# Value products of a sliding-window attention: high and low half of the probabilities in one product of 320 columns, with their results added by VectorE

## Chip, cores and metric

The kernel runs on one core of a Trainium2 chip. The metric is the device time of one launch in microseconds. Six queues of instructions matter: TensorE (PE, with its weight loads as PEld), VectorE (DVE), ScalarE (ACT), GpSimd (POOL) and SyncE (SP), which issues all transfers. They run side by side and wait for each other by semaphores.

## The reference, cut to what matters

The input is 32 sequences of 256 rows of 128 numbers. After a layer norm, two branches are computed and added to the input.

```
h = relu(x @ nm_w1 + nm_b1);  m = h @ nm_w2 + nm_b2
q, k, v = m @ q_w + q_b, m @ k_w + k_b, m @ v_w + v_b
scores = einsum('bsd,bswd->bsw', q, k_band) * scale      # window of 65 rows, 32 to each side
weights = softmax(where(valid, scores, -inf))
attn = einsum('bsw,bswd->bsd', weights, v_band)
combine = top 8 of 16 sigmoid gates, normalised, times 2.826
ffn = sum_e combine[e] * (silu(x @ w_gate[e]) * (x @ w_up[e])) @ w_down[e]  +  shared expert
out = x + attn + ffn
```

## The kernel before

**Tiles.** The 8192 rows are worked in 16 groups of 512 rows, two sequences each. Activations lie turned, 128 features on the partitions and 512 rows on the columns. Every operand of a large product is split in a high part (`_hi`, rounded by ScalarE) and a low part (`_lo`, the rest, by VectorE), and a product is three: hi by hi, lo by hi, hi by lo (`PAIRS3`).

**Slots.** Groups are counted from 0. A group has 17 slots, one for the shared expert and each of the 16 experts. `program` calls `slot(g, par, s)` on every engine in the same order, so the order on an engine is that of its code. In a slot TensorE does `gate_proj` of the next expert into `ps_g`, `down` of the expert three back (`LAG`) into `ps_y`, and `up_proj` of this one into `ps_u`, nine products of 512 columns. ScalarE applies silu (L717), GpSimd multiplies it by the routing weight (`silu_c`, L1257), VectorE multiplies this into `ps_u` (`h_prod`, L1132), ScalarE makes `h_hi` (L725) and VectorE `h_lo` (L1138). `h_prod`, `h_hi` and `h_lo` of an expert are worked in the slot after its own. There are two banks of `ps_u`: `up_proj` of slot s waits for `h_lo` of slot s-2.

**Attention in the slots.** `att_early`, `att_late` and `att` put one piece of the attention in fixed slots. Keys and values need no own projections: the products go to the hidden tile, and value weights are applied after. `hid_n_hi` and `hid_n_lo` (slots 0 and 1) are its two parts with rows on the partitions, reloaded from memory (`store_hid`, `load_hid`; `hid_blocks` in slot 12 of the group before makes the blocks that are stored). `scores` is in slots 3 and 5, the turned probabilities (`prob_hi`, `prob_lo`) are ready in slots 7 to 10. `attend(0)` and `attend(1)` in slots 13 and 14 multiply the hidden tile by them; both sequences of a group write one bank, `bank[2]`. `z_hi` (ScalarE, slot 15) and `z_lo` (VectorE, slot 16) split the result, and `value_proj` adds its product with the value weights to `ps_y` in slot 0 of the next group, or ahead of the last three `down` calls in `finish`.

**What else touches this place.** On VectorE `q_lo` of the next group stands between `z_lo` and `h_lo` of slot 15; the first use of its result is `turn` or `scores` in slots 1 to 3. In slot 1 `hid_n_lo` subtracts two tiles in SBUF. In slot 3 `finish_group` (L1014) reads `ps_y` of the group before, adds the input and signals `s_y_out`; `down` of the new group's first expert, in TensorE's slot 3, waits for that, since it overwrites `ps_y`:

```python
if s == 0 and not first(g):
    pe.wait_ge(s_y_out, g)
```

Of the kernel before, what the change touches and what calls it, by code (L numbers as in the profile page):

```python
# [12 lines left out]
P = 128  # L13
# [59 lines left out]
def layer(nc, x, x_t, watt, watt_t, expert_bias, wexp, out_t, c_dram, st_dram, h_dram):  # L73
    ctx = ExitStack()
    with ctx:
        def sb(name, shape, dt=F32):
            return ctx.enter_context(nc.sbuf_tensor(name, shape, dt))
# [4 lines left out]
        def sem(name):  # L82
# [53 lines left out]


        prob_n = sb("prob_n", [P, NB, 3 * P])
        p_t = [sb("p_hi", [P, NB, 2, SEQ], F32R), sb("p_lo", [P, NB, 2, WIN], F32R)]

# [24 lines left out]
        ps_y = pb("ps_y")  # L167
        bank = [pb(f"bank{i}") for i in range(3)]
        score_bank = [bank[2], bank[1]]


        s_watt_in = sem("watt_loaded")
# [48 lines left out]
            hid_b gate_1 score select top8 rest weight wsum winv comb comb_t  # L221
            hid_mm hid hid_hi hid_lo q_mm q_hi q_lo hid_tp hn_hi hn_lo key_term
            mask_k sc0 sc1 nmax0 nmax1 exp0 exp1 inv0 inv1 pn0 pn1 pt0 pt1
            p0_hi p0_lo p1_hi p1_lo pv z_hi z_lo""".split()
        S = {n: sem(n) for n in names}
        s_hid_st = sem("hid_stored")
        s_hid_m = sem("hid_loaded")
# [20 lines left out]
        def last(g, ahead=0):  # L248
            return g >= GROUPS - 1 - ahead
# [8 lines left out]

        def flat(t):
            return t[:].rearrange("p a d -> p (a d)")  # L260

        def windows(b):

            return b[:, 0:2 * APART].rearrange("p (t c) -> p t c", t=2)[:, :, 0:WIN]
# [139 lines left out]
        def _(pe):  # L404
# [36 lines left out]

            def attend(seq):

                for kb in range(2):
                    col = seq * SEQ + kb * (P - HALF)
                    for n, (a, b) in enumerate(PAIRS3):
                        wide = SEQ if kb == 0 and n == 0 else WIN
                        done = mm(bank[2][:, col:col + wide], hid_n[a][:, seq * 2 + kb, :],  # L448
                                  p_t[b][:, seq, kb, 0:wide], start=kb == 0 and n == 0, stop=kb == 1 and n == 2,
                                  skip_group_check=True)  # L450
                return done

            def value_proj(g):

                pe.wait_ge(S["z_lo"], g + 1)
                for a, b in PAIRS3:
                    mm(ps_y[:], att_w[a][:, 2, :], z_t[b][:], start=False, stop=False, skip_group_check=True)  # L457
# [154 lines left out]
            def att_late(g, par, s):  # L612

                if s == 0 and not first(g):
                    value_proj(g - 1)
                if s == when(g, 9, 12):
                    pe.wait_ge(S["pn1"], g + 1)
                    turn_probs(1)
                if s == 13:
                    pe.wait_ge(S["hn_lo"], g + 1)  # L620
                    pe.wait_ge(S["p0_lo"], g + 1)
                    attend(0)
                if s == 14:
                    pe.wait_ge(S["p1_lo"], g + 1)
                    attend(1).then_inc(S["pv"], 1)

            def slot(g, par, s):
# [19 lines left out]
                        hid_proj(g + 1, 1 - par)  # L647

            def finish():
                value_proj(GROUPS - 1)  # L650
                for s in range(STEPS - LAG, STEPS):
                    down(GROUPS - 1, (GROUPS - 1) % 2, s)

            program(prologue, slot, finish)

        @block.scalar
        def _(act):
# [39 lines left out]

            def z_hi(g):
                act.wait_ge(S["pv"], g + 1)
                A(z_t[0][:], bank[2][:], ACT.Copy).then_inc(S["z_hi"], 1)  # L700

            def prob_exp(g, seq):
                act.wait_ge(S[f"nmax{seq}"], g + 1)
# [5 lines left out]

            def prob_hi(g, seq):  # L710
                act.wait_ge(S[f"pt{seq}"], g + 1)
                A(p_t[0][:, seq, :, 0:WIN], windows(score_bank[seq]), ACT.Copy).then_inc(S[f"p{seq}_hi"], 1)

            def gate_silu(g, par, s):
                i = (par + s) % 2
# [101 lines left out]
        def _(dve):  # L817
# [149 lines left out]

            def z_lo(g):
                dve.wait_ge(S["z_hi"], g + 1)
                V.tensor_tensor(z_t[1][:], bank[2][:], z_t[0][:].bitcast(F32), ALU.subtract).then_inc(S["z_lo"], 1)  # L970

            def prologue():
                V.memset(spin_in[:].bitcast(F32), 0.0).then_inc(s_spin, 1)
                V.memset(prob_n[:], 0.0)
                V.memset(p_t[0][:, :, 0, WIN:SEQ].bitcast(F32), 0.0)
                moments(0, 0)
                variance(0)
                dve.wait_ge(s_gatew_hi, 1)
                V.tensor_tensor(gate_w[:, :, E:2 * E], gate_raw, gate_w[:, :, 0:E].bitcast(F32),
                                ALU.subtract).then_inc(s_gatew, 1)  # L980
                normalise(0, 0)
                xn_lo(0, 0)
                dve.wait_ge(s_attw_hi, 1)
                V.tensor_scalar(vecs[:, 0:1], bank[2][:, M_VEC:M_VEC + 1], att_raw[:, QB:QB + 1], SCALE,
                                ALU.add, ALU.mult)
                V.tensor_scalar(vecs[:, 3:4], bank[2][:, M_VEC + 1:M_VEC + 2], att_raw[:, KB:KB + 1], SCALE,
                                ALU.add, ALU.mult)
                V.tensor_tensor(vecs[:, 1:3], bank[2][:, M_VEC + 1:M_VEC + 3], att_raw[:, KB:VB + 1], ALU.add)\
                    .then_inc(s_vec1, 1)
                V.tensor_tensor(att_w[1][:, 0, :], att_raw[:, W1:W1 + P], att_w[0][:, 0, :].bitcast(F32),  # L990
                                ALU.subtract)
                V.tensor_tensor(att_w[1][:, 2, :], bank[2][:, M_V:M_V + P], att_w[0][:, 2, :].bitcast(F32),
                                ALU.subtract).then_inc(s_attw, 1)
                gate_sum(0)
                route_scores(0)
                route_max(0)
                route_match(0)
                route_sum(0)
                route_weights(0, 0)

                dve.wait_ge(s_side, 1)
                V.tensor_copy(vecs[:, 4:7], ps_u[1][:, M_VEC + 4:M_VEC + 7]).then_inc(s_vec2, 1)
# [35 lines left out]

            def prob_lo(g, seq):
                dve.wait_ge(S[f"p{seq}_hi"], g + 1)  # L1040
                V.tensor_tensor(p_t[1][:, seq, :, :], windows(score_bank[seq]),
                                p_t[0][:, seq, :, 0:WIN].bitcast(F32), ALU.subtract).then_inc(S[f"p{seq}_lo"], 1)

            def att(g, par, s):
                more = not last(g)
# [52 lines left out]
                        hid_lo(g + 1)  # L1098
                if s == 16:
                    z_lo(g)  # L1100
                    if more:
                        q_lo(g + 1)

            def fresh_att(s):

# [35 lines left out]
            def slot(g, par, s):  # L1141
                some = not first(g) or s > 0
                if s == 3 and not first(g):
                    finish_group(g - 1, 1 - par)
                if s == when(g, 6, 9):
                    row_max(g, 1)
                if first(g) and s == 3:
                    score_weights()
                if some:
                    h_prod(*before(g, par, s))  # L1150
                att(g, par, s)
                if some:
                    h_lo(*before(g, par, s))
                if first(g) and s == 1:
                    moments(1, 1)

            def finish():
                h_prod(GROUPS - 1, (GROUPS - 1) % 2, STEPS - 1)
# [153 lines left out]
```

## Time and profile before

| | |
|---|---|
| median of 3 runs | 691.51 us (691.34 to 692.12) |
| the profiled execution | 691.06 us |
| its span | 689.2 us |
| mean granted TensorE clock | 0.997 |
| PE busy | 678.9 us, 98% |
| DVE busy | 596.4 us, 87% |
| ACT busy | 438.2 us, 64% |
| POOL busy | 443.2 us, 64% |

Busy shares are averages over the span. The end of a product is modelled, and consecutive ones overlap in the record: a product of 512 columns is listed with 0.39 us though the next starts 0.23 us after it. So starts are compared, not durations. The same holds for VectorE, where an operation of 512 columns is listed with 0.68 us and the next starts after 0.60.

### The profile page before, as it was taken

Reading aid. Unit: us, or ns where it says so; the run is one execution under the profiler, and the core shown is the slowest. Engines: PE = TensorE matmul, PEld = TensorE weight load, DVE = VectorE, ACT = ScalarE, POOL = GpSimd, SP = SyncE. Lnnn points to the kernel's source line nnn. Section 1 sums busy time; section 2 is a strip of 40 time slices with the busy share of each in tenths; the row PEclk is TensorE's granted clock in tenths of the full one; section 3 lists DMA queues with packets and bytes.
Section 4 is the critical chain, followed back from the end, with each engine's and each line's share of the span. In section 5 each row is a group of like instructions: output and inputs, shape, how many; then the busy total and the mean of one; then the engine's idle time right before and its main releaser. Section 6 shows DMA issues by size and latency. Waiting matters only on the chain.

```text
span 689.2 us, 10454 instructions
## 1 busy us (share of the span) xinstructions
PE 678.9 (98%) x3172; PEld 554.3 (80%) x3172; DVE 596.4 (87%) x1640; ACT 438.2 (64%) x874; POOL 443.2 (64%) x400
## 2 busy tenths in 40 slices
PE   8989999999999999999999999999999999999997
PEld 6768788888888888888888888888888888888886
DVE  7998889988898888889988898888889988888775
ACT  5765665757566566665757566576665757566573
POOL 5774567567666766667567666766667567666553
PEclk9999999999999999999999999999999999999999
DMA  8506246171542626245171643626245161631500
GB/s 268 230 0 250 89 144 225 38 270 62 197 172 94 237 70 248 90 146 223 39 271 62 211 159 92 239 70 263 75 148 221 39 270 46 211 128 63 230 0 16
DMA packets 38040, 101.80 MB, mean 148 GB/s; under 512 B 8672, under 2 KB 18144, under 8 KB 29920
## 3 DMA queue, kind: packets, MB, share of 16 engines
q1 hardware_dynamic: 37984, 101.14, 40.6%
q8 instruction: 25, 0.41, 0.3%
q14 instruction: 31, 0.25, 0.1%
HBM read 92.42 MB, written 8.70 MB: 147 GB/s over the span
## 4 chain that ended last, share of the span: by engine, by line
PE 88%; DVE 5%; ACT 2%; DMA 2%; issue 1%; POOL 0%; SPq 0%; DVEq 0%; ACTq 0%
PE ps_y L487 25%; PE ps_u L477 25%; PE ps_g L467 25%; PE bank L409 3%; PE bank L448 3%; PE bank L431 3%; PE ps_y L457 1%; PE bank L438 1%; DVE ps_u L1132 1%; PE bank L420 1%; DMA h_dram<-exp_raw 1%; PE ps_u L509 1%; DVE h_lo L1138 1%; ACT h_hi L725 1%; ACT silu L717 0%
## 5 line engine op out<-in xcount | busy, mean ns | idle before, releaser
L1257 POOL TENSOR_TENSOR silu_c<-silu,comb_b 128x512 f32<-128x512 f32 x252 | 325.3, 1293 | 226.3 <-ACT silu L717 225.3
L725 ACT ACTIVATE h_hi<-ps_u 128x512 fp32r<-128x512 f32 x272 | 162.6, 598 | 236.1 <-DVE ps_u L1132 236.1
L1138 DVE TENSOR_TENSOR h_lo<-ps_u,h_hi 128x512 fp32r<-128x512 f32 x272 | 185.6, 682 | 40.6 <-ACT h_hi L725 34.7
L1132 DVE TENSOR_TENSOR ps_u<-silu_c,ps_u 128x512 f32<-128x512 f32 x256 | 175.9, 687 | 28.2 <-PE ps_u L477 24.2
L717 ACT ACTIVATE silu<-ps_g 128x512 f32<-128x512 f32 x272 | 161.9, 595 | 0.2
L477 PE MATMUL ps_u<-xn_hi,exp_w_hi 128*128 128x512 f32 x272 | 111.1, 408 | 2.9 <-DVE h_lo L1138 2.8
L487 PE MATMUL ps_y<-h_hi,exp_w_hi 128*128 128x512 f32 x272 | 109.5, 403 | 1.0 <-DVE h_lo L1138 0.4
L467 PE MATMUL ps_g<-xn_hi,exp_w_hi 128*128 128x512 f32 x272 | 108.2, 398 | 0.8 <-ACT silu L717 0.7
L487 PE MATMUL ps_y<-h_lo,exp_w_hi 128*128 128x512 f32 x272 | 107.8, 396 | 0.0
L477 PE MATMUL ps_u<-xn_hi,exp_w_lo 128*128 128x512 f32 x272 | 107.5, 395 | 0.0
L487 PE MATMUL ps_y<-h_hi,exp_w_lo 128*128 128x512 f32 x272 | 107.2, 394 | 0.0
L467 PE MATMUL ps_g<-xn_hi,exp_w_lo 128*128 128x512 f32 x272 | 106.9, 393 | 0.0
L477 PE MATMUL ps_u<-xn_lo,exp_w_hi 128*128 128x512 f32 x272 | 106.6, 392 | 0.0
L467 PE MATMUL ps_g<-xn_lo,exp_w_hi 128*128 128x512 f32 x272 | 105.9, 389 | 0.0
L477 PEld LDWEIGHTS ps_u<-xn_hi,exp_w_hi 128*128 128x128 f32 x272 | 51.1, 188 | 16.7 <-DVE h_lo L1138 5.5
L467 PEld LDWEIGHTS ps_g<-xn_hi,exp_w_hi 128*128 128x128 f32 x272 | 51.1, 188 | 13.5 <-issue 1.1
L487 PEld LDWEIGHTS ps_y<-h_hi,exp_w_lo 128*128 128x128 f32 x272 | 51.3, 189 | 12.4
L467 PEld LDWEIGHTS ps_g<-xn_hi,exp_w_lo 128*128 128x128 f32 x272 | 51.1, 188 | 12.5
L467 PEld LDWEIGHTS ps_g<-xn_lo,exp_w_hi 128*128 128x128 f32 x272 | 51.3, 188 | 12.2
L477 PEld LDWEIGHTS ps_u<-xn_hi,exp_w_lo 128*128 128x128 f32 x272 | 51.1, 188 | 12.2
L487 PEld LDWEIGHTS ps_y<-h_hi,exp_w_hi 128*128 128x128 f32 x272 | 51.3, 189 | 11.4 <-DVE h_lo L1138 0.8
L487 PEld LDWEIGHTS ps_y<-h_lo,exp_w_hi 128*128 128x128 f32 x272 | 51.4, 189 | 9.9
(156 smaller groups left out, 987.8 us busy)
## 6 DMA issues: line engine op xcount, KB each, us to landing
comb_b<-c_dram SPq DMA_DIRECT2D x63, 1024.0 KB, 7.2
mom_b<-st_dram SPq DMA_DIRECT2D x13, 512.0 KB, 3.7
xres<-x_t SPq DMA_DIRECT2D x16, 256.0 KB, 2.5
out_t<-xres SPq DMA_DIRECT2D x16, 256.0 KB, 2.0
xin<-x SPq DMA_DIRECT2D x15, 256.0 KB, 3.1
h_dram<-exp_raw SPq DMA_DIRECT2D x60, 64.0 KB
exp_raw<-h_dram SPq DMA_DIRECT2D x15, 256.0 KB, 3.1
xn<-x_t SPq DMA_DIRECT2D x13, 256.0 KB, 3.4
```

The source lines that it names most:

```text
L409: done = mm(dst[:], att_w[a][:, w, :], parts[b][:], start=n == 0, stop=n == 2)
L420: done = mm(bank[0][:], gate_w[:].rearrange("p q c -> p (q c)"), xn_t[par][n][:], start=n == 0, stop=n == 1)
L431: done = mm(dst[:, t * SEQ:t * SEQ + WIN], q_t[a][:, q0:q0 + P], hid_t[b][:, k0:k0 + WIN], start=n == 0, stop=n == 2)
L448: done = mm(bank[2][:, col:col + wide], hid_n[a][:, seq * 2 + kb, :], p_t[b][:, seq, kb, 0:wide], start=kb == 0 and n == 0, stop=kb == 1 a ...
L467: done = mm(ps_g[i][:], exp_w[a][:, s, 0:P], xn_t[par][b][:], start=n == 0, stop=n == 2)
L477: done = mm(ps_u[i][:], exp_w[a][:, s, P:2 * P], xn_t[par][b][:], start=n == 0, stop=n == 2)
L487: done = mm(ps_y[:], exp_w[a][:, s, 2 * P:3 * P], h_t[i][b][:], start=s == 0 and n == 0, stop=s == STEPS - 1 and n == 2, skip_group_check= ...
L717: A(silu[i][:], ps_g[i][:], ACT.Silu).then_inc(s_silu, 1)
L725: A(h_t[hbuf(par, s)][0][:], ps_u[(par + s) % 2][:], ACT.Copy).then_inc(s_h_hi, 1)
L1132: V.tensor_tensor(ps_u[i][:], src[:], ps_u[i][:], ALU.mult).then_inc(s_h, 1)
L1138: V.tensor_tensor(t[1][:], ps_u[(par + s) % 2][:], t[0][:].bitcast(F32), ALU.subtract)\
L1257: G.tensor_tensor(silu_c[i][:], silu[i][:], comb_b[:, s1 - 1, :], ALU.mult).then_inc(s_silu_c, 1)
```

## The change

Both halves of the probabilities now lie in one tile, `p_t[:, half, sequence, block, :]`. In `attend`, the high part of the hidden tile is multiplied by both halves in one product of 2 x 160 columns. The result of the low half goes to columns 256 to 511 of the same bank, beside that of the high half. The low part of the hidden tile is multiplied by the high half as before. So each sequence needs a bank of its own (`att_bank`), and the second one waits for `hid_hi` of the next group, which reads `bank[0]`. The first product is no longer widened to 256 columns over zeros. ScalarE copies z in two pieces. VectorE subtracts in two pieces, waits for itself, and adds the other half in two more. `q_lo` of the next group moves from between `z_lo` and `h_lo` to the end of slot 16. In `finish`, `value_proj` goes behind the first of the last three `down` calls.

```diff
-        p_t = [sb("p_hi", [P, NB, 2, SEQ], F32R), sb("p_lo", [P, NB, 2, WIN], F32R)]
+        p_t = sb("p_t", [P, 2, NB, 2, WIN], F32R)
...
+        att_bank = [bank[2], bank[0]]
...
+        def halves(b):
+            return b[:].rearrange("p (h t) -> p h t", h=2)
...
             def attend(seq):
+                dst = att_bank[seq]
                 for kb in range(2):
-                    col = seq * SEQ + kb * (P - HALF)
-                    for n, (a, b) in enumerate(PAIRS3):
-                        wide = SEQ if kb == 0 and n == 0 else WIN
-                        done = mm(bank[2][:, col:col + wide], hid_n[a][:, seq * 2 + kb, :],
-                                  p_t[b][:, seq, kb, 0:wide], start=kb == 0 and n == 0, stop=kb == 1 and n == 2,
-                                  skip_group_check=True)
+                    c = slice(kb * (P - HALF), kb * (P - HALF) + WIN)
+                    mm(halves(dst)[:, :, c], hid_n[0][:, seq * 2 + kb, :], p_t[:, :, seq, kb, :],
+                       start=kb == 0, stop=False, skip_group_check=True)
+                    done = mm(dst[:, c], hid_n[1][:, seq * 2 + kb, :], p_t[:, 0, seq, kb, :],
+                              start=False, stop=kb == 1, skip_group_check=True)
...
                 if s == 14:
                     pe.wait_ge(S["p1_lo"], g + 1)
+                    pe.wait_ge(S["hid_hi"], g + 1 + (not last(g)))
                     attend(1).then_inc(S["pv"], 1)
...
             def finish():
-                value_proj(GROUPS - 1)
                 for s in range(STEPS - LAG, STEPS):
                     down(GROUPS - 1, (GROUPS - 1) % 2, s)
+                    if s == STEPS - LAG:
+                        value_proj(GROUPS - 1)
...
             def z_hi(g):
                 act.wait_ge(S["pv"], g + 1)
-                A(z_t[0][:], bank[2][:], ACT.Copy).then_inc(S["z_hi"], 1)
+                for seq in range(NB):
+                    done = A(z_t[0][:, seq * SEQ:(seq + 1) * SEQ], att_bank[seq][:, 0:SEQ], ACT.Copy)
+                done.then_inc(S["z_hi"], 1)
...
             def z_lo(g):
                 dve.wait_ge(S["z_hi"], g + 1)
-                V.tensor_tensor(z_t[1][:], bank[2][:], z_t[0][:].bitcast(F32), ALU.subtract).then_inc(S["z_lo"], 1)
+                for seq in range(NB):
+                    c = slice(seq * SEQ, (seq + 1) * SEQ)
+                    done = V.tensor_tensor(z_t[1][:, c], att_bank[seq][:, 0:SEQ], z_t[0][:, c].bitcast(F32),
+                                           ALU.subtract)
+                done.then_inc(S["z_rest"], 1)
+                dve.wait_ge(S["z_rest"], g + 1)
+                for seq in range(NB):
+                    c = slice(seq * SEQ, (seq + 1) * SEQ)
+                    done = V.tensor_tensor(z_t[1][:, c], att_bank[seq][:, SEQ:2 * SEQ], z_t[1][:, c].bitcast(F32),
+                                           ALU.add)
+                done.then_inc(S["z_lo"], 1)
...
-                V.memset(p_t[0][:, :, 0, WIN:SEQ].bitcast(F32), 0.0)
...
                 if s == 16:
                     z_lo(g)
-                    if more:
-                        q_lo(g + 1)
...
+                if s == STEPS - 1 and not last(g):
+                    q_lo(g + 1)
```

On TensorE, one call of `attend` in slot 13 stands like this before, between the last product of `down` and the first of `up_proj`:

```order
L487 MATMUL ps_y<-h_hi,exp_w_lo 128x512
L448 MATMUL bank<-p_hi,hid_n_hi 128x256 [waits p0_lo,hn_lo]
L448 MATMUL bank<-p_lo,hid_n_hi 128x160
L448 MATMUL bank<-p_hi,hid_n_lo 128x160
L448 MATMUL bank<-p_hi,hid_n_hi 128x160
L448 MATMUL bank<-p_lo,hid_n_hi 128x160
L448 MATMUL bank<-p_hi,hid_n_lo 128x160
L477 MATMUL ps_u<-xn_hi,exp_w_hi 128x512 [waits h_lo_ready]
```

In the changed kernel the same place on TensorE is this:

```order
L495 MATMUL ps_y<-h_hi,exp_w_lo 128x512
L455 MATMUL bank<-p_t,hid_n_hi 128x2x160 [waits p0_lo,hn_lo]
L457 MATMUL bank<-p_t,hid_n_lo 128x160
L455 MATMUL bank<-p_t,hid_n_hi 128x2x160
L457 MATMUL bank<-p_t,hid_n_lo 128x160
L485 MATMUL ps_u<-xn_hi,exp_w_hi 128x512 [waits h_lo_ready]
```

Six products became four, two of them of 2 x 160 columns; nothing else moved past them.

On VectorE, the end of a group (slot 16) and the first operation of the next stand like this before; the products named `ps_u<-silu_c,ps_u` are `h_prod`:

```order
L1132 TENSOR_TENSOR ps_u<-silu_c,ps_u 128x512 [waits silu_c_ready,up_prod_ready]
L970 TENSOR_TENSOR z_lo<-bank,z_hi 128x512 [waits z_hi]
L929 SCALAR_TENSOR_TENSOR q_lo<-bank,vecs,q_hi 128x512 [waits q_hi]
L1138 TENSOR_TENSOR h_lo<-ps_u,h_hi 128x512 [waits h_hi_ready]
L1132 TENSOR_TENSOR ps_u<-silu_c,ps_u 128x512 [waits silu_c_ready,up_prod_ready]
```

In the changed kernel:

```order
L1152 TENSOR_TENSOR ps_u<-silu_c,ps_u 128x512 [waits silu_c_ready,up_prod_ready]
L985 TENSOR_TENSOR z_lo<-bank,z_hi 128x256 [waits z_hi]
L985 TENSOR_TENSOR z_lo<-bank,z_hi 128x256
L991 TENSOR_TENSOR z_lo<-bank,z_lo 128x256 [waits z_rest]
L991 TENSOR_TENSOR z_lo<-bank,z_lo 128x256
L1158 TENSOR_TENSOR h_lo<-ps_u,h_hi 128x512 [waits h_hi_ready]
L942 SCALAR_TENSOR_TENSOR q_lo<-bank,vecs,q_hi 128x512 [waits q_hi]
L1152 TENSOR_TENSOR ps_u<-silu_c,ps_u 128x512 [waits silu_c_ready,up_prod_ready]
```

One operation became four, and `q_lo` went behind `h_lo`, but is still ahead of the next `h_prod`.

## Rows read from the trace of the kernel before

**Rows 1.** The page's first part: busy time of each engine.

```profile
PE 678.9 (98%) x3172; PEld 554.3 (80%) x3172; DVE 596.4 (87%) x1640; ACT 438.2 (64%) x874; POOL 443.2 (64%) x400
```

**Rows 2.** Waits: us in total, times, longest us.

```profile
PE ps_u L477 <- DVE h_lo L1138: 2.8, 4, 1.9
```

**Rows 3.** Timeline of PE, group 6, slot 13: start us, duration us, instruction.

```profile
302.95 0.39 PE L487 MATMUL ps_y<-h_hi,exp_w_lo 128*128 128x512 f32 x1
303.18 0.28 PE L448 MATMUL bank<-p_hi,hid_n_hi 128*128 128x256 f32 x1
303.30 0.23 PE L448 MATMUL bank<-p_lo,hid_n_hi 128*128 128x160 f32 x1
...
303.71 0.28 PE L448 MATMUL bank<-p_hi,hid_n_lo 128*128 128x160 f32 x1
303.82 0.43 PE L477 MATMUL ps_u<-xn_hi,exp_w_hi 128*128 128x512 f32 x1
304.08 0.39 PE L477 MATMUL ps_u<-xn_lo,exp_w_hi 128*128 128x512 f32 x1
```

**Rows 4.** Timeline of ACT, group 1, slot 0: idle time ahead, in brackets.

```profile
66.16 0.63 ACT L696 ACTIVATE hid_n_hi<-exp_raw 128x512 fp32r<-128x512 f32 x1 [2.05 <-DMA exp_raw<-h_dram]
```

**Rows 5.** Timeline of DVE, slot 16 of group 6 to slot 3 of group 7.

```profile
310.29 0.69 DVE L1132 TENSOR_TENSOR ps_u<-silu_c,ps_u 128x512 f32<-128x512 f32 x1 [0.73 <-PE ps_u L477]
310.89 0.68 DVE L970 TENSOR_TENSOR z_lo<-bank,z_hi 128x512 fp32r<-128x512 f32 x1
311.49 0.74 DVE L929 SCALAR_TENSOR_TENSOR q_lo<-bank,vecs,q_hi 128x512 fp32r<-128x512 f32 x1
312.15 0.68 DVE L1138 TENSOR_TENSOR h_lo<-ps_u,h_hi 128x512 fp32r<-128x512 f32 x1
312.75 0.68 DVE L1132 TENSOR_TENSOR ps_u<-silu_c,ps_u 128x512 f32<-128x512 f32 x1
...
315.15 0.70 DVE L1132 TENSOR_TENSOR ps_u<-silu,ps_u 128x512 f32<-128x512 f32 x1 [0.36 <-PE ps_u L477]
315.76 0.77 DVE L949 TENSOR_TENSOR hid_n_lo<-exp_raw,hid_n_hi 128x512 fp32r<-128x512 f32 x1
...
317.00 0.68 DVE L1138 TENSOR_TENSOR h_lo<-ps_u,h_hi 128x512 fp32r<-128x512 f32 x1
...
319.56 0.74 DVE L1014 SCALAR_TENSOR_TENSOR xres<-ps_y,vecs,xres 128x512 f32<-128x512 f32 x1
```

**Rows 6.** Line L1041, a narrower operation: duration ns min/median/max.

```profile
L1041 DVE TENSOR_TENSOR p_lo<-bank,p_hi x32: 472/476/482, 50.9 to 668.2; 128x320 fp32r<-128x320 f32 x32
```

**Rows 7.** Timeline and line L949: GpSimd's product, and subtractions in SBUF.

```profile
304.59 1.30 POOL L1257 TENSOR_TENSOR silu_c<-silu,comb_b 128x512 f32<-128x512 f32 x1 [0.61 <-ACT silu L717]
...
305.35 1.09 DVE L924 TENSOR_TENSOR hid_lo<-hid,hid_hi 128x512 fp32r<-128x512 f32 x1
...
314.70 1.29 POOL L1257 TENSOR_TENSOR silu_c<-silu,comb_b 128x512 f32<-128x512 f32 x1 [1.85 <-ACT silu L717]
...
L949 DVE TENSOR_TENSOR hid_n_lo<-exp_raw,hid_n_hi x15: 691/780/787, 66.8 to 646.5; 128x512 fp32r<-128x512 f32 x15
```

**Rows 8.** Timeline of PE, slots 2 and 3: first products of up_proj and down(0).

```profile
318.44 0.40 PE L477 MATMUL ps_u<-xn_hi,exp_w_hi 128*128 128x512 f32 x1
...
320.46 0.43 PE L487 MATMUL ps_y<-h_hi,exp_w_hi 128*128 128x512 f32 x1
```

**Rows 9.** Timeline of group 1, slot 3: the same place where PE waited.

```profile
70.54 0.74 DVE L1014 SCALAR_TENSOR_TENSOR xres<-ps_y,vecs,xres 128x512 f32<-128x512 f32 x1
...
71.33 0.51 PE L487 MATMUL ps_y<-h_hi,exp_w_hi 128*128 128x512 f32 x1 [0.34 <-DVE xres L1014]
```

**Rows 10.** Timeline of the last 10 us.

```profile
681.53 0.68 DVE L970 TENSOR_TENSOR z_lo<-bank,z_hi 128x512 fp32r<-128x512 f32 x1
...
682.29 0.69 DVE L1138 TENSOR_TENSOR h_lo<-ps_u,h_hi 128x512 fp32r<-128x512 f32 x1
...
684.99 0.50 PE L487 MATMUL ps_y<-h_hi,exp_w_hi 128*128 128x512 f32 x1 [0.37 <-DVE h_lo L1138]
```

More of the change, by code:

```diff
@@ L223, in layer @@
             mask_k sc0 sc1 nmax0 nmax1 exp0 exp1 inv0 inv1 pn0 pn1 pt0 pt1
-            p0_hi p0_lo p1_hi p1_lo pv z_hi z_lo""".split()
+            p0_hi p0_lo p1_hi p1_lo pv z_hi z_rest z_lo""".split()
         S = {n: sem(n) for n in names}
@@ L711, in prob_hi @@
                 act.wait_ge(S[f"pt{seq}"], g + 1)
-                A(p_t[0][:, seq, :, 0:WIN], windows(score_bank[seq]), ACT.Copy).then_inc(S[f"p{seq}_hi"], 1)
+                A(p_t[:, 0, seq, :, :], windows(score_bank[seq]), ACT.Copy).then_inc(S[f"p{seq}_hi"], 1)
             def gate_silu(g, par, s):
@@ L1040, in prob_lo @@
                 dve.wait_ge(S[f"p{seq}_hi"], g + 1)
-                V.tensor_tensor(p_t[1][:, seq, :, :], windows(score_bank[seq]),
-                                p_t[0][:, seq, :, 0:WIN].bitcast(F32), ALU.subtract).then_inc(S[f"p{seq}_lo"], 1)
+                V.tensor_tensor(p_t[:, 1, seq, :, :], windows(score_bank[seq]),
+                                p_t[:, 0, seq, :, :].bitcast(F32), ALU.subtract).then_inc(S[f"p{seq}_lo"], 1)
             def att(g, par, s):
```

## The prediction

> **What bounds the kernel now.** I read the page's busy times, then the waits, then the timeline. TensorE is busy 98% of the span [rows 1], and its second-most frequent direct wait, that of up_proj for h_lo, is 2.8 us in four places [rows 2]. So in nearly every group TensorE's own queue sets the time, and a microsecond taken out of that queue is one gained, as long as VectorE, ScalarE and GpSimd, which prepare its operands, keep their lead. The prediction is therefore two questions: what the value products cost TensorE, and how much of VectorE's lead the longer z work uses up.
>
> **Value products.** One call of attend, in group 6, starts at 303.18. The first product after it starts at 303.82, and the second at 304.08 [rows 3]. A product of 512 columns has a pitch (start to start) of 0.23 there (302.95 to 303.18) [rows 3], so the call costs 304.08 - 303.18 - 0.23 = 0.67 us. Its 256-column product has a pitch of 0.12, and a 160-column one 0.11 (303.71 to 303.82) [rows 3], although by columns it should be 0.07: each product loads its own weights, and these loads follow each other no faster. After the change a call is 320, 160, 320, 160 columns. A 320-column product is in no row; between 256 columns at 0.12 and 512 at 0.23 it comes to 0.145 (an estimate). The 160-column ones stay at 0.11. So a call costs 2 x (0.145 + 0.11) = 0.51, and saves about 0.155 us. Bounds: 0.12 for the wide product (the narrower row) saves 0.21 per call, and 0.23 (the wider row) saves nothing. I take the straight line, since the two rows differ by their columns alone.
>
> The Trainium skill (TensorE: Matmul & The Clock Gate, Back-to-back issue gap) gives an isolated product N/2.4 + 2.5 ns. By that alone a call would go from 0.46 to 0.41 and save 0.045 us. The row has 0.67 for the call, so here the loads count too, which the same section says of a stream of loads and products.
>
> Thirty-two calls are made. The two of group 0 I count at nothing: in group 1, slot 1, ScalarE waits 2.05 us for the reloaded hidden tile, from memory [rows 4], whose transfer hangs on hid_blocks in slot 12, ahead of those calls, and TensorE waits behind it. Gain: 30 x 0.155 = 4.7 us.
>
> **The z block on VectorE (slot 16).** Before, it is one subtraction of 512 columns with a pitch of 0.60 (310.89 to 311.49) and a duration of 0.68, then q_lo with a pitch of 0.66 [rows 5]. After, it is four of 256 columns, the third waiting for the second to end. A 320-column operation of the same kind lasts 476 ns [rows 6] against 683, so 256 columns last about 0.41, with a pitch of 0.33 (the overlap of 0.08 with the next stays). The block is 0.33 + 0.41 + 0.03 + 0.33 + 0.33 = 1.43; 0.03 is the own semaphore, an estimate below the 0.05 that TensorE takes after VectorE's end [rows 9]. That is +0.83 per group. Bounds: each of the four at the 320-column pitch of 0.40 gives +1.11, and at half the 512-column pitch, 0.30, gives +0.71. The z copies of ScalarE become two; z_lo at 310.89 finds them done, so they hide.
>
> q_lo moves behind h_lo(15). So h_lo(15) starts only 0.17 later, well before its reader, but h_prod(16) at 312.75 is behind both and starts 0.83 later, at 313.58. q_lo's reader, scores(0) in slot 3, is far off. The memset of p_hi that goes from the prologue is counted at nothing, since VectorE waits for x there.
>
> **Where the 0.83 goes.** Before slot 16's z block VectorE had waited 0.73 for TensorE [rows 5], so up to there it keeps step with the faster TensorE. From h_prod(16) on, everything is late by 0.83: h_hi(16), then silu(1) behind it on ScalarE, then GpSimd's silu_c(1) at 314.70, whose idle time ScalarE's silu ended [rows 7]. VectorE itself had 0.36 idle before h_prod(0) at 315.15 [rows 5] and would win back 0.45 there (the overlap of 0.08 too). But hid_n_lo follows, with both inputs in SBUF, and it doesn't run beside GpSimd's product: it lasts 0.77 from 315.76 to 316.53, which is 0.54 after GpSimd's end at 315.99. hid_lo shows the same: 1.09 long, its end at 306.44 is 0.55 after GpSimd's end at 305.89. Alone, hid_n_lo lasts 691 ns at its least [rows 7]. So its end is tied to GpSimd's end and not to its own start: it is late by the full 0.83, and with it the VectorE queue behind it.
>
> The Trainium skill (SBUF — State Buffer, Who interferes with whom) says that a VectorE instruction with two SBUF inputs and a GpSimd one that reads SBUF block each other fully, first come first served. By that rule the delay passes on, as by these rows.
>
> **What TensorE then waits for.** h_lo(0) starts at 317.00 [rows 5]; late by 0.83 and 0.68 long it ends at 318.51. up_proj(2) waits for it, started at 318.44 [rows 8], and can start at 318.56: 0.12 late. A product that had to wait is also longer, 0.51 in the waiting case [rows 9] against 0.40 [rows 8], since its weights came late: 0.23 in all. Then finish_group, which must read ps_y before down(0) of the new group may overwrite it: xres starts at 319.56 and takes 0.74 [rows 5], so it ends at 320.30, and down(0) starts at 320.46 [rows 8]. With 0.05 for the semaphore the lead is 0.11 us. Late by 0.83, xres ends at 321.13, down(0) starts at 321.18, 0.72 later than now, and with 0.51 for 0.43 the loss is 0.80 (the earlier 0.23 is in it, since both count from the same delayed queue). Group 1 shows this wait already: xres at 70.54, down(0) at 71.33, 0.34 idle [rows 9]; there VectorE was free for want of the transfer, which hides the 0.83. That leaves the 14 boundaries before groups 2 to 15. After slot 4 TensorE, itself late, is waited for again, and nothing is carried into the next group. Loss: 14 x 0.80 = 11.2 us.
>
> **The end.** The last group has no q_lo. z_lo starts at 681.53 and h_lo(15) at 682.29 [rows 10]; after, 681.53 + 1.43 = 682.96. h_prod(16), h_hi(16), h_lo(16) and the last down follow in line (it waits 0.37 for h_lo at 684.99 [rows 10]): +0.67. value_proj behind the first down has cover until then.
>
> **Sum.** -4.7 + 11.2 + 0.7 = +7.2 us. The profiled execution took 691.06 (span 689.2), the median of the three runs is 691.51, 0.45 above it, so the run becomes 698.3 and the median 698.7 us, 1.0% slower.
>
> **Rivals.**
> - *The delay isn't inherited through GpSimd.* If hid_n_lo runs beside silu_c(1), VectorE wins back 0.45 at h_prod(0) and is late by 0.38. Then up_proj(2) doesn't wait, and down(0) loses 0.38 - 0.11 + 0.08 = 0.35. Sum: -4.7 + 4.9 + 0.7 = +0.9, 692.4 us. Against it are 14 stretched hid_n_lo. Chance 0.12.
> - *Faster.* VectorE's delay at finish_group stays under the lead of 0.11 us. It decides there and nowhere else: below it no boundary costs anything and the products' gain is left, -4.7 + 0.7 = -4.0, 687.5 us. For it: VectorE is idle 13% of the span, some of it in slots 1 to 4, and the price of a 256-column operation is read from wider ones. Against it: even at the lower bound of +0.71 and with 0.45 won back, 0.26 is left. Chance 0.13.
> - *The wide product saves nothing.* Two separate stretches of 160 columns in one product could cost as two, 0.22. A call is then 0.66, the gain is nil: +11.9, 703.4 us. Nothing in the trace reads or writes columns in two such pieces on TensorE at this width, so it isn't excluded. Chance 0.12. By the skill's gap alone, the gain would be 30 x 0.045 = 1.4 and the time 702.
> - *The forecast*, one boundary loss near 0.8 and a call near 0.51: chance 0.6. Its own range is 696 to 702: the bounds of the z block move it by -0.12 x 14 = -1.7 and +0.28 x 14 = +3.9, those of the product by -1.7.
> - 0.03 for something above all of these.
>
> **Chances.** A difference under 0.2%, 1.4 us, can't be told from none: 690.1 to 692.9. Faster is the second rival, 0.13. Same is the first rival, most of it, 0.10. Slower is the rest, 0.77. The range leaves out the faster case and the extreme ends: 692.0 to 703.5.
>
> **What the profile after would show.** (1) attend: starts 0.145 and 0.11 apart, a call at 0.51. (2) Four z operations near 410 ns, h_prod(16) 0.83 later against the up_proj(16) before it. (3) hid_n_lo stretched from 0.77 to about 1.2. (4) In the waits, TensorE at ps_y's first product for xres in 15 groups, where it is one now, and for h_lo at up_proj(2); the step from up_proj(2) to down(0) longer. (5) The last wait for h_lo near 1.0 in place of 0.37. It would be wrong if hid_n_lo's end isn't tied to GpSimd, if the delay is taken up before slot 3 by some idle time that I didn't count, or if the 320-column product isn't priced by its columns.

## The result, and the profile after

| | before | changed |
|---|---|---|
| median | 691.55 us (691.34 to 692.12, 4 runs) | 713.19 us (712.66 to 713.32, 4 runs) |
| span of the profiled execution | 689.2 us | 710.8 us |
| granted TensorE clock | 0.997 | 0.997 |

The changed kernel is slower by 3.1%: the ratio is 1.031, 95% interval 1.0292 to 1.0328. The forecast was 698.7 us, range 692.0 to 703.5. The direction was right, and the loss is three times as large as forecast.

The page's first part, after, against [rows 1]: TensorE's busy time hardly moved, VectorE's rose by 32.5 us (the page shows rounded shares).

```profile
PE 680.9 (96%) x3108; PEld 549.9 (77%) x3108; DVE 628.9 (88%) x1687; ACT 439.0 (62%) x890; POOL 442.1 (62%) x400
```

The waits after, against [rows 2]: us in total, times, longest us. The wait of `up_proj` for `h_lo` had 2.8 us in 4 places, and the one of `down` for `xres` is now in 15 groups.

```profile
PEld ps_u L485 <- DVE h_lo L1158: 26.3, 23, 2.3
PE ps_u L485 <- DVE h_lo L1158: 16.9, 17, 1.9
PEld ps_y L495 <- DVE xres L1036: 7.3, 15, 0.5
PE ps_y L495 <- DVE xres L1036: 5.0, 15, 0.3
```

The timeline of TensorE after, group 6, slot 13, the place of [rows 3]. A 320-column product has a pitch of 0.14 and 0.19, a 160-column one of 0.07. The call, counted as before, is 311.49 - 310.74 - 0.23 = 0.52 us (0.51 forecast, 0.67 before).

```profile
310.51 0.39 PE L495 MATMUL ps_y<-h_hi,exp_w_lo 128*128 128x512 f32 x1
310.74 0.31 PE L455 MATMUL bank<-p_t,hid_n_hi 128*128 128x320 f32 x1
310.88 0.23 PE L457 MATMUL bank<-p_t,hid_n_lo 128*128 128x160 f32 x1
310.95 0.35 PE L455 MATMUL bank<-p_t,hid_n_hi 128*128 128x320 f32 x1
311.14 0.24 PE L457 MATMUL bank<-p_t,hid_n_lo 128*128 128x160 f32 x1
311.21 0.44 PE L485 MATMUL ps_u<-xn_hi,exp_w_hi 128*128 128x512 f32 x1
311.49 0.39 PE L485 MATMUL ps_u<-xn_lo,exp_w_hi 128*128 128x512 f32 x1
```

VectorE's timeline after, slot 16 of group 6 to slot 3 of group 7, as [rows 5]. From `h_prod(15)` at 317.51 to `h_prod(16)` at 320.82 are 3.31 us, 2.46 before: +0.85, forecast +0.83. `hid_n_lo` lasts 1.24, forecast "about 1.2". What wasn't forecast is the second `key_prod` behind it, 1.36 us long; the first took 0.34.

```profile
317.51 0.70 DVE L1152 TENSOR_TENSOR ps_u<-silu_c,ps_u 128x512 f32<-128x512 f32 x1 [0.72 <-PE ps_u L485]
318.11 0.75 DVE L985 TENSOR_TENSOR z_lo<-bank,z_hi 128x256 fp32r<-128x256 f32 x2
318.90 0.76 DVE L991 TENSOR_TENSOR z_lo<-bank,z_lo 128x256 fp32r<-128x256 f32 x2
...
320.82 0.69 DVE L1152 TENSOR_TENSOR ps_u<-silu_c,ps_u 128x512 f32<-128x512 f32 x1
...
322.78 0.68 DVE L1152 TENSOR_TENSOR ps_u<-silu,ps_u 128x512 f32<-128x512 f32 x1
323.38 1.24 DVE L962 TENSOR_TENSOR hid_n_lo<-exp_raw,hid_n_hi 128x512 fp32r<-128x512 f32 x1
324.54 0.34 DVE L975 CUSTOM_DVE_ANT_0 key_prod<-exp_raw,key_row,vecs 128x128 f32<-128x128 f32 x1
...
324.81 1.36 DVE L975 CUSTOM_DVE_ANT_0 key_prod<-exp_raw,key_row,vecs 128x128 f32<-128x128 f32 x1
...
326.10 0.68 DVE L1158 TENSOR_TENSOR h_lo<-ps_u,h_hi 128x512 fp32r<-128x512 f32 x1
...
327.57 0.34 DVE L975 CUSTOM_DVE_ANT_0 key_prod<-exp_raw,key_row,vecs 128x128 f32<-128x128 f32 x1
...
328.05 0.69 DVE L1158 TENSOR_TENSOR h_lo<-ps_u,h_hi 128x512 fp32r<-128x512 f32 x1
328.66 0.74 DVE L1036 SCALAR_TENSOR_TENSOR xres<-ps_y,vecs,xres 128x512 f32<-128x512 f32 x1
```

GpSimd's timeline in the same stretch shows what stands beside both; that it is the cause is for the experiments to show. `silu_c(1)` ends at 324.06 and `hid_n_lo` 0.56 after it. `silu_c(2)` starts at 324.66, 0.15 ahead of the second `key_prod` and 0.12 behind the first; it ends at 326.02, and the stretched one at 326.17.

```profile
322.77 1.29 POOL L1279 TENSOR_TENSOR silu_c<-silu,comb_b 128x512 f32<-128x512 f32 x1 [2.71 <-ACT silu L730]
324.66 1.36 POOL L1279 TENSOR_TENSOR silu_c<-silu,comb_b 128x512 f32<-128x512 f32 x1 [0.60 <-ACT silu L730]
```

TensorE's timeline at the two places of [rows 8], both without a wait before:

```profile
326.84 0.50 PE L485 MATMUL ps_u<-xn_hi,exp_w_hi 128*128 128x512 f32 x1 [1.01 <-DVE h_lo L1158]
...
329.46 0.50 PE L495 MATMUL ps_y<-h_hi,exp_w_hi 128*128 128x512 f32 x1 [0.33 <-DVE xres L1036]
```

I worked out a table from the same timelines: the step from the start of one slot's `up_proj` to the next, median over groups 4 to 14, and its difference to the kernel before, in us. It is used for every run below. Slots that aren't listed differ by 0.01 at most in this run.

| step | before | changed | |
|---|---|---|---|
| slot 1 to 2 | 2.087 | 3.270 | +1.183 |
| slot 2 to 3 | 2.761 | 3.428 | +0.667 |
| slot 12 to 13 | 2.720 | 2.563 | -0.157 |
| slot 13 to 14 | 2.753 | 2.587 | -0.166 |
| group | 41.347 | 42.865 | +1.518 |

The account of the spans closes: -0.37 up to the start of group 2, 13 groups up to that of group 15 +19.77, group 15 to its last `up_proj` +1.51, from there to the end +0.69. Sum +21.6, and 710.8 - 689.2 = 21.6.

### The profile page after: what moved, and what is told of

Same layout as the page of the kernel before. It is cut to its first block, busy times and chain, and to the rows that moved or that the text cites. A ratio compares the mean times of both kernels' runs of the same rounds, so it can differ in the third digit from the quotient of the medians.

```text
span 710.8 us, 10405 instructions
## 1 busy us (share of the span) xinstructions
PE 680.9 (96%) x3108; PEld 549.9 (77%) x3108; DVE 628.9 (88%) x1687; ACT 439.0 (62%) x890; POOL 442.1 (62%) x400
## 4 chain that ended last, share of the span: by engine, by line
PE 65%; DVE 22%; issue 6%; ACT 5%; DMA 2%; POOL 0%; SPq 0%; DVEq 0%; ACTq 0%
PE ps_y L495 19%; PE ps_u L485 19%; PE ps_g L475 17%; DVE ps_u L1152 6%; DVE key_prod L975 3%; ACT h_hi L738 3%; PE bank L417 3%; DVE h_lo L1158 2%; DVE xres L1036 2%; DVE q_lo L942 2%; DVE hid_n_lo L962 1%; DVE z_lo L985 1%; PE bank L455 1%; PE bank L446 1%; PE bank L439 1%
## 5 line engine op out<-in xcount | busy, mean ns | idle before, releaser
L485 PE MATMUL ps_u<-xn_hi,exp_w_hi 128*128 128x512 f32 x272 | 112.7, 414 | 17.2 <-DVE h_lo L1158 16.9
```

The lines of the kernel that those rows point to most:

```text
L485: done = mm(ps_u[i][:], exp_w[a][:, s, P:2 * P], xn_t[par][b][:], start=n == 0, stop=n == 2)
```

## The experiments

Theory A: VectorE operations that can't run beside GpSimd's product turn 0.85 us of delay into 1.9, and the gain of the products is there but smaller. Theory B has a different explanation in each run, given there. Theory C: the larger amount of VectorE work alone makes the loss. Every run was timed beside runs of the kernel before, and its ratio is to these; intervals are 95%.

### The z block alone, and the products alone

`e1_z_block_only` is the kernel before with VectorE's part of the change; the additions go to a tile that nobody reads, so their work stands but not their result.

```diff
+                done.then_inc(S["z_rest"], 1)
+                dve.wait_ge(S["z_rest"], g + 1)
...
+                    done = V.tensor_tensor(z_pad[:, c], bank[2][:, c], z_t[1][:, c].bitcast(F32), ALU.add)
...
+                if s == STEPS - 1 and not last(g):
+                    q_lo(g + 1)
```

> The kernel before with VectorE's side of the change alone: z_lo in two subtractions of 256 columns, the own wait, two additions of 256 columns (into a scratch tile, so the result stays), and q_lo behind h_lo(15). The value products stay the six of before. Theory A (the longer z block makes VectorE late, and GpSimd's products then stand in the way of its operations with two SBUF inputs in slot 1): all of the loss and none of the gain, 713.2 + 4.7 = about 717.9 us. Rival B (the loss comes from the products, the second bank or its wait on hid_hi): near the kernel before, at most 692.4 to 698.7 us.

Measured: 718.33 us (717.98 to 718.92), ratio 1.0381 [1.0366, 1.0397]. All of the loss is here (14 x 1.85 + 0.7 = 26.6 us by the steps), with nothing changed on TensorE or ScalarE. That rules out the new products, the second bank and the wait for `hid_hi` as its cause.

`e2_no_addition` is the changed kernel without the two additions and their wait; the low half's contribution to z is left out.

```diff
-                done.then_inc(S["z_rest"], 1)
-                dve.wait_ge(S["z_rest"], g + 1)
...
-                    V.tensor_tensor(z_t[1][:, c], att_bank[seq][:, SEQ:2 * SEQ], z_t[1][:, c].bitcast(F32),
-                                           ALU.add)
```

> The changed kernel without the two additions of z's low half (the low half of the probabilities doesn't reach the result) and without the wait between. TensorE's and ScalarE's side stay. Theory A: the z block has a pitch of 0.67 in place of 0.60, nothing is late, and the gain of the products stands alone, 691.5 - 4.7 = about 687 us. Rival B (products, bank or the wait on hid_hi): stays above 700 us.

Measured: 688.77 us (688.71 to 690.5), ratio 0.9961 [0.9947, 0.9975]. Its steps are -0.157 and -0.166 in slots 13 and 14, as in the changed kernel, and +0.134 from slot 2 to 3: the two pieces and the moved `q_lo` still make VectorE late enough for `xres`. That remainder is 14 x 0.134 = 1.9 us, and it is why this run isn't at 687.

### The same work, met by GpSimd at another time

`e3_q_lo_slot0` moves `q_lo` behind `h_lo(16)` in slot 0. VectorE does the same work up to `xres`.

```diff
-                if s == STEPS - 1 and not last(g):
-                    q_lo(g + 1)
+                if s == 0 and not first(g):
+                    q_lo(g)
```

> The changed kernel with q_lo of the next group moved from the end of slot 16 to the end of slot 0, behind h_lo(16). VectorE's work is the same. h_prod(16), ScalarE's silu(1) and GpSimd's silu_c(1) are then late by about 0.2 us and not 0.85, while hid_n_lo starts as late as now. Theory A: hid_n_lo no longer waits for GpSimd, the key products go through before silu_c(2), h_lo(0) is late by 0.3 us, down(0) costs about 0.3 us at 14 boundaries: about 691.5 us. Rival C (the amount of VectorE's work between slot 16 and slot 3 sets it, whatever GpSimd does): as the changed kernel, 713 us.

Measured: 691.23 us (690.91 to 691.96), ratio 0.9992 [0.9983, 1.0001]. 22 us are gone with one operation moved by a slot. `hid_n_lo` begins 0.05 us ahead of the end of GpSimd's product and lasts 0.69, and the key products last 0.35. Left is +0.277 from slot 2 to 3. `xres` comes 0.31 later than before, and this remainder is what the amount of work costs. So theory C is ruled out for the 22 us.

`e5_half_silu_c` is the changed kernel with GpSimd's product of experts 1 and 2 on half of the columns (the other half of the columns of these two experts' contribution is left out).

```diff
-                    G.tensor_tensor(silu_c[i][:], silu[i][:], comb_b[:, s1 - 1, :], ALU.mult).then_inc(s_silu_c, 1)
+                    n = T // 2 if s1 <= 2 else T
+                    G.tensor_tensor(silu_c[i][:, 0:n], silu[i][:, 0:n], comb_b[:, s1 - 1, 0:n], ALU.mult)\
+                        .then_inc(s_silu_c, 1)
```

> The changed kernel with GpSimd's silu_c product of experts 1 and 2 of each group cut to 256 columns (the other half of the columns keeps old values, so the result is not the reference's). VectorE, ScalarE and TensorE do all that they did. Theory A: hid_n_lo ends 0.55 after GpSimd's shorter product, the second key product meets no GpSimd product, h_lo(0) comes 1.5 us earlier, TensorE waits only 0.3 us at down(0): about 691.5 us. Rival C (VectorE's own work sets it): 713 us, since nobody waits for these two GpSimd products.

Measured: 691.49 us (690.95 to 691.78), ratio 0.9991 [0.9982, 1.0001]. VectorE's program is untouched, and about 22 us go when GpSimd's operation is shorter. It lasts 0.74 in place of 1.30 and `hid_n_lo` ends 0.55 earlier than in the changed kernel (medians against `up_proj(0)`), though it starts where it did; the key products last 0.34. Left is +0.279 from slot 2 to 3. VectorE didn't wait for GpSimd's result as an operand: that wait is 4.0 us in 15 places in the kernel before and in the changed one alike.

### Only the key product out of the way

`e6_key_slot2` puts the first two key products in slot 2, and the mask terms on GpSimd that read them one slot later. `e10_key_slot2_alone` has only the first pair of lines below and leaves the mask terms in slot 2.

```diff
-                if s == when(g, 1, 5):
+                if s == when(g, 2, 5):
                     key_terms(g, 0)
-                if s == when(g, 2, 5):
+                if s == when(g, 3, 5):
                     mask_terms(g, 0)
```

> The changed kernel with the first pair of key products in slot 2 instead of slot 1 (and the mask terms that read it one slot later), so that no key product stands where GpSimd's next product begins. VectorE's operations are the same and as many; up to xres in slot 3 the same work lies before it. Theory A (the second key product is locked out by GpSimd's product of expert 2, 1.36 in place of 0.34, and this was missing in my sum): the key products last 0.34 each, only hid_n_lo stays stretched at about 1.24, VectorE is late by about 0.83 as forecast, and the time is near the forecast's, 696 to 701 us. Theory C (VectorE's amount of work alone makes the loss): xres comes as late as before this edit and the time stays at 713 us.

Measured: 717.10 us (716.73 to 717.47), ratio 1.0372 [1.0354, 1.0389], outside both expectations. My edit had brought a wait of its own, that of `row_max` in slot 4 for the mask:

```profile
DVE prob L1045 <- POOL mask_k L1263: 30.1, 15, 2.0
```

The steps separate it: 0.000 from slot 1 to 2, where the changed kernel has +1.183, +0.644 from slot 2 to 3, and then +0.403, +0.535, +0.256, +0.011, +0.022 and +0.082 in slots 5 to 11. So I ran it again without that wait.

> As the run with the first key products in slot 2, but with GpSimd's mask terms left in slot 2, so that row_max doesn't wait for them. That run's steps of TensorE from up_proj to up_proj (medians over groups 4 to 14, against the kernel before) were 0 from slot 1 to 2, where the changed kernel has +1.18, +0.64 from slot 2 to 3, and +1.2 in slots 5 to 10, where row_max waited 2.0 us for the mask. Theory A: the last of these goes and the others stay, so a group is -0.33 + 0.64 = +0.31 against before, 14 x 0.31 + 0.7 at the end = +5.0: 695 to 698 us, which is the forecast's own case. Theory C (amount of work): 713 us.

Measured: 696.26 us (696.2 to 696.47), ratio 1.0069 [1.0054, 1.0084]. The steps are -0.001 from slot 1 to 2 and +0.638 from slot 2 to 3. With the key product out of the way of GpSimd's next one, the change costs +4.7 us in place of +21.6. That is close to the forecast's case, but not the same, since two key products have also moved behind `h_prod(1)`. `hid_n_lo` is as stretched as ever (duration ns min/median/max), and the wait for `xres` is TensorE's only new one:

```profile
L962 DVE TENSOR_TENSOR hid_n_lo<-exp_raw,hid_n_hi x15: 692/1247/1249, 67.1 to 651.1; 128x512 fp32r<-128x512 f32 x15
```

```profile
PEld ps_y L495 <- DVE xres L1036: 8.9, 15, 0.9
...
PE ps_y L495 <- DVE xres L1036: 6.6, 15, 0.8
```

### Two doses of delay in the kernel before

One VectorE operation of 128 or of 384 columns is added ahead of `z_lo`, in every group but the last.

```diff
+                if not last(g):
+                    V.tensor_tensor(z_pad[:, 0:128], bank[2][:, 0:128], z_t[0][:, 0:128].bitcast(F32), ALU.add)
                 V.tensor_tensor(z_t[1][:], bank[2][:], z_t[0][:].bitcast(F32), ALU.subtract).then_inc(S["z_lo"], 1)
```

> The kernel before with one extra operation of 128 columns on VectorE ahead of z_lo in slot 16 of every group but the last, written to a tile that nobody reads: a delay of about 0.2 us (an estimate: below the 0.33 of 256 columns). The second key product then still begins ahead of GpSimd's next product (316.73 + 0.2 against 317.05). Theory A: only the lead at xres of 0.11 is used up, 14 x (0.2 - 0.11 + 0.08) = 2.4, 693 to 695.5 us, and no key product is stretched. Theory B (a delay at VectorE costs a multiple of itself wherever it is put): 14 x 0.2 x 2.2 = 6, 697 us or more.

> The same with 384 columns, a delay of about 0.46 us (between 0.40 for 320 and 0.60 for 512 columns). The second key product would begin at 317.19, behind GpSimd's product at 317.05. Theory A: there is a step between the two doses, not a slope: the key product is locked out and gains a further 1.0 us of delay, 14 x (0.46 + 1.02 - 0.11 + 0.1) = 20.6, 708 to 713 us. Theory B (a slope): 14 x (0.46 - 0.11 + 0.08) = 6.0, 697 to 699 us if it costs once, 705 if it costs twice.

| | delay of `h_prod(16)` | step 1 to 2 | step 2 to 3 | us | ratio |
|---|---|---|---|---|---|
| 128 columns | 0.20 | 0.000 | +0.179 | 694.30 | 1.0040 [1.0025, 1.0055] |
| 384 columns | 0.46 | +0.814 | +0.664 | 712.76 | 1.0305 [1.0287, 1.0322] |

The delays are medians of the starts against the same group's `up_proj(0)`. The first 0.20 us cost 2.7 us, and 0.26 more cost 18.5, of which a plain delay of 0.26 in 14 groups would be 3.6. The lines of `hid_n_lo` and `key_prod` (ns min/median/max) with 128 columns:

```profile
L950 DVE TENSOR_TENSOR hid_n_lo<-exp_raw,hid_n_hi x15: 691/990/991, 67.3 to 649.5; 128x512 fp32r<-128x512 f32 x15
```

```profile
L963 DVE CUSTOM_DVE_ANT_0 key_prod<-exp_raw,key_row,vecs x60: 336/344/350, 67.9 to 652.4; 128x128 f32<-128x128 f32 x60
```

and the timelines of VectorE and of GpSimd there, group 6:

```profile
275.64 0.99 DVE L950 TENSOR_TENSOR hid_n_lo<-exp_raw,hid_n_hi 128x512 fp32r<-128x512 f32 x1
...
276.83 0.34 DVE L963 CUSTOM_DVE_ANT_0 key_prod<-exp_raw,key_row,vecs 128x128 f32<-128x128 f32 x1
```

```profile
274.78 1.30 POOL L1260 TENSOR_TENSOR silu_c<-silu,comb_b 128x512 f32<-128x512 f32 x1 [2.05 <-ACT silu L718]
276.94 1.39 POOL L1260 TENSOR_TENSOR silu_c<-silu,comb_b 128x512 f32<-128x512 f32 x1 [0.86 <-ACT silu L718]
```

With 384 columns, the same two timelines:

```profile
282.46 0.34 DVE L963 CUSTOM_DVE_ANT_0 key_prod<-exp_raw,key_row,vecs 128x128 f32<-128x128 f32 x1
...
282.73 1.38 DVE L963 CUSTOM_DVE_ANT_0 key_prod<-exp_raw,key_row,vecs 128x128 f32<-128x128 f32 x1
```

```profile
282.58 1.38 POOL L1260 TENSOR_TENSOR silu_c<-silu,comb_b 128x512 f32<-128x512 f32 x1 [0.59 <-ACT silu L718]
```

At 128 columns the second key product begins 0.11 ahead of GpSimd's product and lasts 0.34. At 384 it begins 0.15 behind it and lasts 1.38. That is a step, no slope: in all 14 groups of the first run the second key product lasts 0.34 or 0.35, in all 14 of the other 1.37 or 1.38.

### Towards a better version

`e7_hid_n_lo_slot4` moves `hid_n_lo` to slot 4, `e8_both_moved` does this and the edit of `e3_q_lo_slot0`, `e9_before_hid_n_lo_slot4` does it in the kernel before. `e11_three_moved` adds to `e8_both_moved` the second pair of key products in slot 3 and its mask terms in slot 4.

```diff
-                if s == when(g, 1, 4):
-                    hid_n_lo(g)
...
+                if s == when(g, 4, 4):
+                    hid_n_lo(g)
```

> The changed kernel with hid_n_lo in slot 4 instead of slot 1 (its only reader is attend in slot 13). q_lo stays in slot 16, so the 0.83 us of delay goes into slot 0 as it does now. Theory A (the delay costs TensorE only through the operations that exclude GpSimd's product, and through the lead at xres): without hid_n_lo the key products run at 0.34 or one is stretched by a few tenths, xres is no later than in the kernel before, both waits at the boundary go or stay below 0.2 us, and the gain of the value products shows: 686 to 690 us. Theory C (the delay at h_prod(16) itself costs, whatever stands in slot 1): 14 boundaries still lose some 0.8 each, 698 us or more.

> The changed kernel with q_lo at the end of slot 0 and hid_n_lo in slot 4: the candidate for a version that beats both. With q_lo alone moved 691.23 us was measured, with a wait of TensorE for xres left at each boundary (0.13 to 0.14 between two products longer than without it, and a late weight load). Theory A: with hid_n_lo out of the way that wait goes too and TensorE's queue alone is left, 684 to 688 us. If the time stays at 691, the wait at the boundary has another cause than VectorE's work ahead of xres.

> The kernel before with hid_n_lo in slot 4 alone: what the lead of 0.11 us at xres and the stretched hid_n_lo cost the kernel before. By its trace TensorE waited for xres in one group only, so theory A expects almost nothing, 690 to 691.5 us; the distance to the run with both moved is then the pure worth of the value products, 30 x about 0.155 = 4.7 us less what is left of the z block at the end (0.7). If this run falls by several us too, the kernel before was held by VectorE more than its waits view shows.

> The version with q_lo in slot 0 and hid_n_lo in slot 4 (689.13 us), and in addition the second pair of key products in slot 3 and its mask terms in slot 4. In the version's trace the step of TensorE from slot 2 to 3 was still 0.087 longer than in the kernel before, with a key product of 0.77 in slot 2. Theory A: this goes, 14 x 0.087 = 1.2 us, 687.5 to 688.5 us. If instead TensorE waits somewhere in slots 3 to 5 for VectorE, it stays at 689 or more.

| | us | ratio | steps that differ from before (slots 13 and 14 apart; above 0.01) |
|---|---|---|---|
| e7 | 693.64 | 1.0031 [1.0017, 1.0044] | 2 to 3 +0.164, 7 to 8 +0.190, 8 to 9 +0.012, 9 to 10 +0.022, 10 to 11 +0.086 |
| e8 | 689.13 | 0.9964 [0.9952, 0.9976] | 2 to 3 +0.087 |
| e9 | 691.93 | 1.0003 [0.9994, 1.0013] | none |
| e11 | 690.90 | 0.9990 [0.9980, 0.9999] | 7 to 8 +0.082, 8 to 9 +0.014, 9 to 10 +0.023, 10 to 11 +0.089 |

`e8_both_moved` is the changed kernel's products with a schedule that bears them: 2.5 us below the kernel before. That is a smaller gain than the 684 to 688 I expected. A wait for `xres` was left, since a key product of slot 2 is stretched to 0.77 us; of the products' 14 x 0.332 = 4.6 us, 14 x 0.087 = 1.2 and the end's 0.7 go off, which leaves 2.7.

`e7_hid_n_lo_slot4` missed its range: its `hid_n_lo` lasts 1.17 in slot 4, again beside a GpSimd product, and there is a new loss in slots 7 to 11. That the one makes the other isn't shown: `e11_three_moved` has steps in the same slots with a `hid_n_lo` of 0.68. `e9_before_hid_n_lo_slot4`, at 0.4 us above its range, gains nothing, although `down(0)` now starts 0.42 after the end of `xres` in place of 0.15: the kernel before had no loss there. `e11_three_moved` missed its range by 2.4 us: it did remove the step from slot 2 to 3, as expected, but lost in slots 7 to 11, where `up_proj` waits for `h_lo` in more places (weight loads 21 times, 8 in `e8_both_moved`). Which of VectorE's operations makes these late was not tested.

## Why the prediction was right in direction and wrong in size

- **The products: right.** A call at 0.52 against 0.51. The steps from slot 12 to 15 give 0.157 + 0.166 + 0.009 = 0.332 a group, 4.6 us in 14 groups; forecast 0.31 a group and 4.7 in all. The pitches inside the call were off, and the closeness of the sum is partly luck: the narrow products have 0.07 and not 0.11, the wide ones 0.14 and 0.19 and not 0.145, together 0.47 in place of 0.51, and the 512-column product behind them gives 0.05 back.
- **The z block: right.** +0.85 against +0.83, and +0.69 at the end against +0.67 (last `up_proj` to the end of the span).
- **The inheritance through GpSimd: right, now shown by the doses.** With 128 columns `hid_n_lo` starts where it did (1.50 after `up_proj(0)` in both) but ends 0.21 later, 0.55 after GpSimd's end (276.63 against 276.08). It is not its start that counts. The Trainium skill (SBUF — State Buffer, Who interferes with whom) states mutual blocking for such a pair, first come first served; these durations and `e5_half_silu_c` agree.
- **The lead at `xres`: right.** The delay of `xres`, less the lead of 0.11, plus 0.08 gives the measured step from slot 2 to 3 within 0.01 us in `e2_no_addition`, `e3_q_lo_slot0`, `e5_half_silu_c`, `e7_hid_n_lo_slot4` and `e12_delay_128` (for instance 0.31 - 0.11 + 0.08 = 0.28 against +0.277).
- **The failed step:** "it is late by the full 0.83, and with it the VectorE queue behind it". I passed 0.83 on unchanged from `hid_n_lo` to `h_lo(0)`. Two key products stand between them, and they read SBUF too. Before, the second began 0.32 ahead of GpSimd's next product (316.73 against 317.05, rows below). After, VectorE was late by 0.86 there, but GpSimd's next product by 0.40 only: its `silu(2)` stands on ScalarE behind `h_hi(0)`, which waits for `h_prod(0)`, and there VectorE had won back 0.45, as the prediction says. So the lead became 0.32 + 0.40 - 0.86 = -0.14, and the product waited for GpSimd: 1.36 in place of 0.34. So the delay at `h_lo(0)` is 0.86 + 1.02 = 1.88 and not 0.83. With it the forecast's own formula gives 1.88 - 0.11 + 0.08 = 1.85 per boundary in place of 0.80; measured is 1.183 + 0.667 = 1.85. The term "14 x 0.80 = 11.2" measures 14 x 1.85 = 25.9.
- **No second miss hides in this term.** `e10_key_slot2_alone` lost 0.64 a boundary and not the forecast's 0.80, but by its own edit. In the kernel before, VectorE has 0.21 us to spare ahead of `h_lo(1)`: the last key product starts at 318.47, with a pitch of 0.27 as the others have (316.46 to 316.73), and `h_lo(1)` starts at 318.95 and not at 318.74 (rows below), behind `h_hi(1)`, which ScalarE ends at 318.92. In the changed kernel this gap is still there (327.57 + 0.27 = 327.84, and 328.05), since `h_prod(1)` and `h_hi(1)` are as late as the rest: `h_lo(0)`, `h_lo(1)` and `xres` are all late by 1.88. In `e10_key_slot2_alone` the two moved key products fill it, and `xres` is late by 0.68.
- **The rivals.** None of the three happened. No rival of mine allowed a second collision, and so the range ended at 703.5; only the chance of 0.03 for something above covered it. A rival "the next SBUF operation meets GpSimd's next product" would have set 0.32 us of lead, and the 0.4 by which `h_prod(0)` and with it GpSimd's product move, against 0.83 of delay, at a price of 14 x 1.0.

The rows of the kernel before that the prediction doesn't use, VectorE's and GpSimd's timelines in slots 1 and 2 of group 7:

```profile
316.46 0.34 DVE L962 CUSTOM_DVE_ANT_0 key_prod<-exp_raw,key_row,vecs 128x128 f32<-128x128 f32 x1
...
316.73 0.34 DVE L962 CUSTOM_DVE_ANT_0 key_prod<-exp_raw,key_row,vecs 128x128 f32<-128x128 f32 x1
...
318.47 0.34 DVE L962 CUSTOM_DVE_ANT_0 key_prod<-exp_raw,key_row,vecs 128x128 f32<-128x128 f32 x1
...
318.95 0.69 DVE L1138 TENSOR_TENSOR h_lo<-ps_u,h_hi 128x512 fp32r<-128x512 f32 x1
```

```profile
317.05 1.30 POOL L1257 TENSOR_TENSOR silu_c<-silu,comb_b 128x512 f32<-128x512 f32 x1 [1.06 <-ACT silu L717]
```

## What to carry to other kernels

Where two engines exclude each other, a delay isn't passed on as it is. For each operation behind the delayed one, read how far ahead of the other engine's next operation it starts, and add by how much that operation moves itself. This lead is a threshold. Here, once past it, a key product ended 1.02 us later, because GpSimd's product lasts 1.30, and 0.26 us of additional delay cost 18.5 us. Moving one operation by a slot took 22 us off (`e3_q_lo_slot0`). But a moved operation has its own readers and neighbours: `e6_key_slot2` brought a new wait for the mask, and `e7_hid_n_lo_slot4` and `e11_three_moved` lost in slots 7 to 11.

## What was not expected of the hardware

- The custom operation behind `key_prod`, two inputs in SBUF and 128 columns, is held up by GpSimd's product just as a plain subtraction is: 1.36 to 1.38 us in place of 0.34. It ends 0.15 us after GpSimd's recorded end, a subtraction of 512 columns 0.55 after it; both are less than what they last alone (0.34 and 0.69).
- The runs together show this as a curve. Where the key product starts 0.15 us or less before GpSimd's recorded end, it lasts 0.34; where 0.22, 0.34, 0.50, 0.62 and 1.21 before it, 0.37, 0.49, 0.64, 0.77 and 1.36, always 0.14 to 0.15 past that end (medians; `e10_key_slot2_alone`, `e7_hid_n_lo_slot4`, `e9_before_hid_n_lo_slot4`, `e8_both_moved`, changed kernel). `hid_n_lo` does the same: it lasts 0.69 when it starts 0.14 before the end (`e5_half_silu_c`), and 0.78, 0.95, 0.99 and 1.24 when 0.23, 0.40, 0.44 and 0.69 before it (kernel before, `e2_no_addition`, `e12_delay_128`, changed kernel).
- It works in the other direction too, with less at stake. A GpSimd product that starts 0.31 us behind the start of a key product lasts 1.30. One that starts 0.15 or 0.13 behind lasts 1.36, and 0.10 behind 1.40 (kernel before, `e2_no_addition`, changed kernel, `e12_delay_128`), while the key product keeps its 0.34.
- Wide and narrow products in turn have pitches of 0.14 to 0.19 and 0.07, although in [rows 3] a 160-column product beside others had 0.11. What follows pays part of it back: the first 512-column product after the call has a pitch of 0.28 (0.26 before), where other 512-column products have 0.23. No run shows why; in both kernels the weight loads inside the call start 0.11 us apart or more.
